# A mixture-of-experts layer on Trainium2: expert results scatter-added into the output in memory instead of stored as parts and summed in a last stage

## The reference, cut to what matters

```
h = layernorm(x) * (1 + cb) + sb
logits = h @ router_w.T;  topk_w, topk_idx = top_k(softmax(logits), 2);  topk_w /= sum(topk_w)
for e in range(8):
    out += (silu(h @ Wg[e].T) * (h @ Wu[e].T)) @ Wd[e].T * comb[:, e]
x = x + gb * out          # gb: one row of 256 gates per batch
```

## Time and profile before

| what | us |
|---|---|
| median of 3 runs | 319.98 |
| lowest and highest | 319.64, 322.03 |
| the profiled execution, own time | 321.41 |
| the profiled execution, span from first to last instruction | 319.6 |
| mean granted TensorE clock (share of full speed) | 0.873 |

### The profile page before, as it was taken

The page is one execution under the profiler, slowest core; times in us unless marked ns, Lnnn a source line. Parts: engine busy times, 40 slices in busy tenths (PEclk is TensorE's granted clock), DMA queues, the critical chain, the costliest instruction groups (busy, mean ns, idle before and its releaser), DMA issues.

```text
span 319.6 us, 4248 instructions
## 1 busy us (share of the span) xinstructions
PE 248.6 (78%) x1154; PEld 157.7 (49%) x1155; DVE 170.7 (53%) x448; ACT 119.7 (37%) x262; POOL 82.5 (26%) x93
## 2 busy tenths in 40 slices
PE   3889298967452228999997899999999999999500
PEld 0236166656352113666664466666666666666300
DVE  1356805798877972844667244444444444443236
ACT  1158367427828243564453222223232323222000
POOL 0103646531100051022242122223333222211223
PEclk9999859997555556999999799999999999999955
DMA  7993270418072925231011111011010111100083
GB/s 266 362 417 127 71 295 33 180 25 352 2 257 105 301 69 207 91 126 29 33 36 33 33 33 35 21 36 33 17 45 29 33 34 44 33 2 0 0 269 125
DMA packets 12663, 33.88 MB, mean 106 GB/s; under 512 B 2049, under 2 KB 7684, under 8 KB 11624
## 3 DMA queue, kind: packets, MB, share of 16 engines
q1 hardware_dynamic: 10152, 28.51, 24.5%
q0 software_dynamic: 2208, 5.17, 5.5%
q10 hardware_dynamic: 288, 0.02, 0.1%
HBM read 29.45 MB, written 5.14 MB: 108 GB/s over the span
## 4 chain that ended last, share of the span: by engine, by line
PE 68%; DVE 18%; DMA 5%; ACT 4%; issue 3%; SPq 1%; POOL 0%; DVEq 0%; POOLq 0%; ACTq 0%
PE bank L572 27%; PE bank L600 19%; PE bank L584 5%; PE bank L464 4%; PE bank L501 2%; DVE W L873 2%; ACT W L646 2%; PE bank L421 2%; DMA W<-expert_parts 2%; PE bank L477 2%; PE bank L561 2%; DMA x<-in_x 2%; PE bank L489 1%; DMA rows<-token_rows,source_i 1%; PE bank L533 1%
## 5 line engine op out<-in xcount | busy, mean ns | idle before, releaser
L572 PE MATMUL bank<-W,rows 128*128 x414 | 90.2, 374 | 4.2 <-DVE W L873 3.2
L600 PE MATMUL bank<-W,shared 128*128 (+1 forms) x276 | 67.9, 388 | 0.7 <-DVE shared L1067 0.7
L572 PEld LDWEIGHTS bank<-W,rows 128*128 128x128 f16 x414 | 41.6, 101 | 46.8 <-issue 10.4
L1043 DVE SCALAR_TENSOR_TENSOR shared<-bank,unscale,rows 128x256 f32<-128x256 f32 (+1 forms) x69 | 31.7, 461 | 60.7 <-ACT rows L723 56.2
L1142 POOL DMA_INDIRECT expert_parts<-shared,dest_i x23 | 23.3, 1014 | 131.4 <-DVE shared L1052 131.4
L600 PEld LDWEIGHTS bank<-W,shared 128*128 128x128 f32 (+1 forms) x276 | 48.7, 189 | 13.4 <-issue 8.6
L723 ACT ACTIVATE rows<-bank,unscale 128x256 f32<-128x256 f32 (+1 forms) x69 | 31.4, 455 | 51.8 <-PE bank L572 40.9
L1128 POOL DMA_INDIRECT rows<-token_rows,source_i x23 | 25.7, 1118 | 34.9 <-DVE source_i L843 28.2
L646 ACT ACTIVATE W<-staged,w_scale_bits 128x704 f16<-128x704 f32 x32 | 25.9, 870 | 11.7 <-DVE w_scale_bits L863 11.7
L733 ACT ACTIVATE shared<-bank 128x128 f32<-128x128 f32 x23 | 6.4, 277 | 62.1 <-PE bank L584 62.1
L873 DVE SCALAR_TENSOR_TENSOR W<-staged,w_scale_bits,W 128x704 f16<-128x704 f32 x32 | 29.4, 966 | 0.0
(11 more groups left out here) (155 smaller groups left out, 255.6 us busy)
## 6 DMA issues: line engine op xcount, KB each, us to landing
staged<-in_w SPq DMA_DIRECT2D x8, 1408.0 KB, 6.4
W<-in_w SPq DMA_DIRECT2D x8, 768.0 KB, 8.8
W<-expert_parts SPq DMA_DIRECT2D x8, 256.0 KB, 4.8
W<-in_wmod SPq DMA_DIRECT2D x3, 512.0 KB, 7.4
token_rows<-rows SPq DMA_DIRECT2D x1, 1040.0 KB, 5.8
x<-in_x SPq DMA_DIRECT2D x4, 256.0 KB, 8.8
W<-mod_rows SPq DMA_DIRECT2D x4, 256.0 KB, 4.4
out<-x SPq DMA_DIRECT2D x4, 256.0 KB, 2.3
```

The costliest lines, as they stand in the source:

```text
L572: mm = pe.matmul(bank[2 + n][:, 0:2 * w], slot[:, kc * P:(kc + 1) * P], W1_pairs[:, bass.ds(e * 2 + part, 1), :, kc, n * PIECE:n * PIECE + w],
L600: mm = pe.matmul(bank[7][:, 0:D], actT[0:rows, fc * P:(fc + 1) * P], W2[0:rows, bass.ds(e * W2_EXP + fc * D, D)], start=(fc == 0), stop=(f ...
L1043: ve.scalar_tensor_tensor(act[:, n * PIECE:n * PIECE + w], bank[2 + n][:, w:2 * w], unscale[c % 2][:, 1:2], sig[:, n * PIECE:n * PIECE + w ...
```

## The change

Each expert result is multiplied by weight and gate in one VectorE instruction and is then added, by the DMA itself, to the output in memory, which has been filled with the residual `x` beforehand. In detail:

1. The rows of `token_rows` grow from 260 to 516 numbers: behind each token's row stands its batch's gate row (`GATE`). SP writes these four gate blocks from `gate_b` early on, behind a new wait on `gateb_in`. The gathers fetch 516 numbers per slot. Two of the four buffers `xs` now lie in `rows1`, two in `x`.
2. SP writes `x` to `out` (four transfers of 256 KB) once the second normalization is done. POOL's first gather waits for this and for the gate blocks, besides the old waits.
3. `result` becomes a `scalar_tensor_tensor` with the gathered gate as second operand.
4. The scatter goes to `out` with an addition, and each waits until the scatter before it has landed, since two results of one token add to the same row. `out` has 128 rows more: an empty slot of partition p adds to row 1024 + p, and nothing is out of bounds any more. VectorE computes `pad_row` for that.
5. The reload of the parts, `finish` and the four output transfers at the end are gone. The kernel ends when all scatters have landed.

```diff
-        rows_d = nc.dram_tensor("token_rows", (TOKENS, ROW), F32, kind="Internal").ap()
-        parts_d = nc.dram_tensor("expert_parts", (2 * TOKENS, D), F32, kind="Internal").ap()
+        rows_d = nc.dram_tensor("token_rows", (TOKENS, ROW_ALL), F32, kind="Internal").ap()
...
-        xs = [rows1[:, r * ROW:(r + 1) * ROW] for r in range(4)]
+        xs = [rows1[:, r * ROW_ALL:(r + 1) * ROW_ALL] for r in range(2)] + [x[:, r * ROW_ALL:(r + 1) * ROW_ALL] for r in range(2)]
...
+            sp.wait_ge(s["gateb_in"], 16 * B)
+            for b in range(B):
+                gate = gate_b[:, b * (D + 1):b * (D + 1) + D].rearrange("p (a d) -> p a d", a=1)
+                sp.dma_start(rows_d[b * S:(b + 1) * S, GATE:].rearrange("(t p) n -> p t n", p=P),
+                             gate.to_broadcast([P, TB, D])).then_inc(s["gates_out"], 16)
             load_w2(2)
             load_w2(3)
...
+            sp.wait_ge(s["h2_ok"], B)
+            for b in range(B):
+                sp.dma_start(out[b * S:(b + 1) * S].rearrange("(t p) d -> p t d", p=P),
+                             v3(x[:, b * TB * D:(b + 1) * TB * D], TB)).then_inc(s["x2_out"], 16)
             sp.wait_ge(s["rows_ok"], 1)
-            sp.dma_start(rows_d.rearrange("(t p) n -> p t n", p=P), v3(rows1[:], TT)).then_inc(s["rows_out"], 16)
+            sp.dma_start(rows_d[:, 0:ROW].rearrange("(t p) n -> p t n", p=P), v3(rows1[:], TT)).then_inc(s["rows_out"], 16)
...
+            sp.wait_ge(s["x2_out"], 16 * B)
             for r in range(2):
                 sp.wait_ge(y_out[r], 16 * len(range(r, SLOT_TILES, 2)))
-            for b in range(B):
-                for k, part in enumerate((part1, part2)):
-                    sp.dma_start(v3(part[:, b * TB * D:(b + 1) * TB * D], TB),
-                                 parts_d[k * TOKENS + b * S:k * TOKENS + (b + 1) * S].rearrange("(t p) d -> p t d", p=P)
-                                 ).then_inc(part_in[b], 16)
...
+            ve.tensor_scalar(pad_row[:], keep[:, C_TOKEN:C_TOKEN + 1], float(TOKENS), None, ALU.add)
...
-            ve.tensor_scalar(nobody[:], filled[:], 0.5, float(NOWHERE), ALU.is_lt, ALU.mult)
+            ve.tensor_scalar(nobody[:], filled[:], 0.5, pad_row[:, 0:1], ALU.is_lt, ALU.mult)
...
-            link(ve.tensor_tensor(nobody[:], nobody[:], filled[:], ALU.add))
+            link(ve.tensor_tensor(nobody[:], nobody[:], source[:], ALU.add))
...
-                ve.tensor_scalar(y_sb[r], bank[7][:, 0:D], slot_weight[c % 4][:, 0:1], None,
-                                 ALU.mult).then_inc(s["y_ok"], 1)
+                ve.scalar_tensor_tensor(y_sb[r], bank[7][:, 0:D], slot_weight[c % 4][:, 0:1], xs[c % 4][:, GATE:],
+                                        ALU.mult, ALU.mult).then_inc(s["y_ok"], 1)
...
             po.wait_ge(s["rows_out"], 16)
+            po.wait_ge(s["gates_out"], 16 * B)
+            po.wait_ge(s["x2_out"], 16 * B)
             po.wait_ge(s["source_ok"], 1)
...
                 po.wait_ge(s["y_ok"], j + 1)
-                po.indirect_dma_start(parts_d, bass.IndirectOffsetOnAxis(dest_i[:, j:j + 1], 0), y_sb[r], None,
-                                      bounds_check=last_part, oob_is_err=False).then_inc(y_out[r], 16)
+                if j:
+                    po.wait_ge(y_out[1 - r], 16 * ((j + 1) // 2))
+                po.indirect_dma_start(out, bass.IndirectOffsetOnAxis(dest_i[:, j:j + 1], 0), y_sb[r], None,
+                                      bounds_check=last_row, oob_is_err=True, compute_op=ALU.add).then_inc(y_out[r], 16)
```

More of the change, by code:

```diff
@@ L26 @@
 WEIGHT, WEIGHT_STEP, UNSCALE = D, D + 1, D + 2
-NOWHERE = 1 << 20
+GATE = ROW
+ROW_ALL = ROW + D
 PIECE = 256
@@ L238, in layer @@
         dest_i = sb("dest_i", NT, U32)
+        pad_row = sb("pad_row", 1)
         slot_weight = [sb(f"slot_weight{r}", 1) for r in range(4)]
@@ L272, in layer @@
             gu_done sig_ok act_ok xt_done slot_hi_ok slot_lo_ok unscale_ok at_done actT_a actT_v down_done y_ok
-            fin_ok pool_fin_ok out_done""".split()
+            gates_out x2_out""".split()
         s = {n: sem(n) for n in names}
@@ L280, in layer @@
         wmod_in = [sem(f"wmod_in{n}") for n in range(3)]
-        part_in = [sem(f"part_in{b}") for b in range(B)]
         def wait_places(eng, e):
@@ L311, in turns @@
                 step(0, j)
-        def finish(eng, batches, link, done):
-            for b in batches:
-                cols = slice(b * TB * D, (b + 1) * TB * D)
-                eng.wait_ge(part_in[b], 32)
-                link(eng.tensor_tensor(part1[:, cols], part1[:, cols], part2[:, cols], ALU.add))
-                g3 = gate_b[:, b * (D + 1):b * (D + 1) + D].rearrange("p (a d) -> p a d", a=1).to_broadcast([P, TB, D])
-                link(eng.tensor_tensor(v3(part1[:, cols], TB), v3(part1[:, cols], TB), g3, ALU.mult))
-                eng.tensor_tensor(x[:, cols], part1[:, cols], x[:, cols], ALU.add).then_inc(done, 1)
         block = ctx.enter_context(nc.Block())
@@ L388, in _ @@
             load_w1(7)
+            sp.wait_ge(s["x2_out"], 16 * B)
             for r in range(2):
                 sp.wait_ge(y_out[r], 16 * len(range(r, SLOT_TILES, 2)))
-            for b in range(B):
-                for k, part in enumerate((part1, part2)):
-                    sp.dma_start(v3(part[:, b * TB * D:(b + 1) * TB * D], TB),
-                                 parts_d[k * TOKENS + b * S:k * TOKENS + (b + 1) * S].rearrange("(t p) d -> p t d", p=P)
-                                 ).then_inc(part_in[b], 16)
-            for b in FINISH_DVE[:-1] + FINISH_POOL + FINISH_DVE[-1:]:
-                if b in FINISH_POOL:
-                    sp.wait_ge(s["pool_fin_ok"], FINISH_POOL.index(b) + 1)
-                else:
-                    sp.wait_ge(s["fin_ok"], FINISH_DVE.index(b) + 1)
-                sp.dma_start(out[b].rearrange("(t p) d -> p t d", p=P),
-                             v3(x[:, b * TB * D:(b + 1) * TB * D], TB)).then_inc(s["out_done"], 16)
-            sp.wait_ge(s["out_done"], 16 * B)
         @block.tensor
@@ L1073, in _ @@
             result(0, SLOT_TILES - 1, (SLOT_TILES - 1) % 2)
-            ve.wait_ge(s["gateb_in"], 16 * B)
-            finish(ve, FINISH_DVE, link, s["fin_ok"])
         @block.gpsimd
@@ L1131, in _ @@
             last_token = po.to_reg(TOKENS - 1)
-            last_part = po.to_reg(2 * TOKENS - 1)
+            last_row = po.to_reg(TOKENS + P - 1)
             po.wait_ge(s["rows_out"], 16)
+            po.wait_ge(s["gates_out"], 16 * B)
+            po.wait_ge(s["x2_out"], 16 * B)
             po.wait_ge(s["source_ok"], 1)
@@ L1141, in _ @@
                 po.wait_ge(s["y_ok"], j + 1)
-                po.indirect_dma_start(parts_d, bass.IndirectOffsetOnAxis(dest_i[:, j:j + 1], 0), y_sb[r], None,
-                                      bounds_check=last_part, oob_is_err=False).then_inc(y_out[r], 16)
+                if j:
+                    po.wait_ge(y_out[1 - r], 16 * ((j + 1) // 2))
+                po.indirect_dma_start(out, bass.IndirectOffsetOnAxis(dest_i[:, j:j + 1], 0), y_sb[r], None,
+                                      bounds_check=last_row, oob_is_err=True, compute_op=ALU.add).then_inc(y_out[r], 16)
                 if j + 4 < SLOT_TILES:
                     gather(j + 4)
-            po.wait_ge(s["gateb_in"], 16 * B)
-            finish(po, FINISH_POOL, klink, s["pool_fin_ok"])
 _ORDER = ["L0_attn_X", "L0_attn_W_in", "L0_attn_b_in", "L0_attn_W_out", "L0_attn_b_out", "L0_ffn_router_w",
@@ L1163 @@
     args = [nc.dram_tensor(f"in_{n}", a.shape, F32, kind="ExternalInput").ap() for n, a in arrays.items()]
-    out = nc.dram_tensor("out", (B, S, D), F32, kind="ExternalOutput").ap()
+    out = nc.dram_tensor("out", (TOKENS + P, D), F32, kind="ExternalOutput").ap()
     layer(nc, *args, out)
     r = run_bass_kernel_spmd(nc, [{f"in_{n}": a for n, a in arrays.items()}], core_ids=[0])
-    return r.results[0]["out"]
+    return r.results[0]["out"][:TOKENS].reshape(B, S, D)
```

3 lines of the change are left out of this document (removed).

## The result

The changed kernel takes 308.73 us (median of 4 runs, 308.24 to 309.24) against 319.85 for the kernel before in the same comparison: a ratio of 0.9638 of the means, 95% interval 0.9593 to 0.9682, so 10.2 to 13.0 us less. Forecast were 306.6 us and a range of 303.5 to 314. Direction and range held; the forecast point was 2.1 us too low. The profiled execution's own time is 308.24, its span 306.4.

The account below looks back on a forecast made before the run. The prediction took PE to bound the steady part and the last stage the end. Last scatter issued at 301.8, landing 4.0 and closing 0.4 gave span 306.2, 13.4 less; median 306.6 us, range 303.5 to 314.

Parts of the forecast that it names:

- Removed, 15.9 us: End of the kernel: reload, `finish` and output transfers, from 303.28 to 319.2, all on the path, would be saved.
- 0.4 us of closing: End of the kernel: only 0.4 us would follow the last scatter's landing.
- nothing else covers it: End of the kernel: no other work would hide the removed last stage, so its whole 15.9 us would be saved.
- L = 4.0: Adding scatter, issue to landing: 2.1 us plain, 1.3 for a round trip, 0.6 for more bytes.
- The upper bound of 12.5: Adding scatter's issue-to-landing time if each DMA engine took its 8 rows singly, 1.3 us each on top of 2.1.
- The waits, 0: Between scatters: waiting for the earlier landing costs nothing, until landing takes 7.4 us, or 4.52 at the last two.
- First gather, 0.5: Front of the kernel: the first gather, widened to 516 numbers, comes 0.5 us later, bounds 0 and 1.0.
- Gate transfers, 0: Early SP queue: waiting for gates delays down weights 2 and 3 by 6 to 9 us, at no cost.
- Residual to `out`, 0: Before the tiles: writing 1 MB delays ACT's weights 4.0 us, covered by 8.85 us of idling; cost 0, bounds 0 and 3.
- 3: Rival at the front: the residual's 1 MB delays weights or first gather by up to 3 us; median up to 309.6; chance 0.04.
- 1: Rival at the end: landing takes 4.5 to 7.4 us, last two scatters in series; median up to about 313; chance 0.20.
- 2: Rival in the tiles: landing over 7.37 us makes scatters the chain, losing from 7.9, median up to 426; chance 0.10.

Follow-up runs that it names:

- the doubled scatters: Changed kernel with each adding scatter issued twice, the second after the first has landed; ratio 1.0639 against the kernel before, span 339.5 us.
- the memset: Changed kernel with one more POOL instruction at its end, a 128 x 1 memset waiting for the last landing in buffer 0; ratio 0.9712 against the kernel before.

## Why the prediction was right or wrong, point by point

- **Removed, 15.9 us.** As a stretch of the chain it was right; as a saving it was not. It was worth 13.3, shown by the kernel before without its stage. This is the step that failed, in the form "0.4 us of closing" and "nothing else covers it": in the trace of before that 0.4 followed a landing at which POOL had finished its drain, though only by 0.9 us. I carried it over to an end at which POOL works until the last moment. There the time from the last landing to the end was 2.2 us. What a deleted stage covers has to be asked of each engine, the end-of-program instructions included.
- **L = 4.0.** Measured 3.8 (3.7 for the last scatter), but not from the parts that I added. The plain scatter of the same wait structure took 2.4 and not 2.1, and the addition 1.4 more and not 1.9; of these 1.4, 0.57 are descriptors, a term that I had put at nothing. The round trip of 1.3 was not measured by itself. So the closeness is in part luck. The upper bound of 12.5, rows one after another in each DMA engine, is far off. From the last issue to the end it is 5.85 where I had 4.0 + 0.4. This one term is 1.45 us of the 2.1 by which the median lies over the forecast. L entered the result less than in the forecast: 1.4 us more of landing moved the end by 0.8. By the fit above, an estimate, it moves the end only from about 3.5 on, and then one for one.
- **The Trainium skill** (Collectives: The Full Stack, "Why ReduceScatter is half of AllGather") counts twice the reads for an addition. My estimate from that alone, L = 2.4, does not agree with the trace: 3.8. The packets of the transfer took more than three times as long in sum as those of the plain scatter (the view adds up packet times, so its share can exceed 1). In windows of half a microsecond in the changed kernel:

```profile
302.50:303.00 0.50, 0.00 (x0) 0.00 (x0) 0.00 (x0) 0.00 (x0) 0.00 (x0) 0.50 0.76 68
303.00:303.50 0.50, 0.00 (x0) 0.00 (x0) 0.00 (x0) 0.00 (x0) 0.00 (x0) 0.50 1.12 156
303.50:304.00 0.50, 0.00 (x0) 0.00 (x0) 0.00 (x0) 0.00 (x0) 0.00 (x0) 0.50 0.28 39
```

  (0.76 + 1.12 + 0.28) x 0.5 = 1.08 us of packet time per engine for one scatter, against 0.32 for the plain one in the earlier trace rows. "Three times the bytes" in my estimate would be 0.96, so this part was about right.
- **The waits, 0.** Right but for the 0.05 us at the last scatter, by the kernel without them. The thresholds were wrong, for the 0.77 us between a landing and the next issue: 6.6 and not 7.4 in the steady part, 3.75 and not 4.52 at the end.
- **First gather, 0.5.** Measured 0.57.
- **`result`, 0.** Right: 482 ns against 484. `pad_row`: about the 0.1 allowed.
- **Gate transfers, 0.** SP waited 4.0 us for the gate broadcasts and issued the four at 43.79, down weights 2 and 3 at 45.82; gate and up weights 2 went out at 57.23, held by VectorE as before.
- **Residual to `out`, 0.** ACT's wait for the staged weights grew from 1.15 to 3.28 us, so by 2.1 where I had allowed 4.0; its idle time ahead of the next work fell from 8.85 to 6.87. No wait followed on PE:

```profile
101.22 1.38 ACT L620 ACTIVATE W<-staged 128x1408 bf16<-128x1408 f32 x1 [3.28 <-DMA staged<-in_w]
...
114.01 3.20 ACT L628 ACTIVATE W<-staged,w_scale_bits 128x704 f16<-128x704 f32 x4 [6.87 <-DVE w_scale_bits L846]
```

- **The rest of the 2.1 us** is the reference point. The forecast carried the difference between two spans over to the medians. The spans did differ by 13.2 (13.4 forecast) for partly wrong reasons: the profile of before came 1.4 us above its median, and that of the changed kernel was the fastest of its four.
- **The rivals.** 3 did not occur. Of 1 there is only the 0.05 us at the last scatter, with L = 3.8 just past the edge. 2 did not occur, but its mechanism is real: the doubled scatters show it.

## What to carry to other kernels

A stage at the end of the chain is worth its length less whatever ran beside it unseen; look for the engine whose end-of-program instruction comes last once the stage is gone. With dozens of indirect DMAs issued by GpSimd that instruction takes microseconds, and a drain placed in an idle gap of GpSimd, shortly before the end, takes most of it off the path. An adding scatter with serial waits is free while its landing plus 0.8 us fits under the step it lies beside (here 4.6 under 7.37, but no longer under the 4.52 of the last two), and doubling it is a cheap test of how far that is from the edge.

## What the runs showed of the hardware that was not expected

- **GpSimd's final drain grows with the number of indirect DMAs**: 4.1 to 4.3 us from its last work to the end with 46, 5.9 with 69, and 2.6 (hardly more than the landing) with 3 or 2 left after an earlier drain. That its time counts from GpSimd's last work, whatever this is, is shown by the memset; that it also cannot end before the last landing, and ends later the more DMAs there were, is read from the table of drains and was not tried. Nor was what it works off.
- **An adding scatter of 128 rows of 1 KB** costs GpSimd 1.55 to 1.6 us instead of 1.0, lands 3.8 us after its issue instead of 2.4, and has 1.08 us of packet time per DMA engine instead of 0.32.
- **The first part scatters by several microseconds with TensorE's clock.** The first gather was issued between 113.4 and 118.1 us. In the nine profiles with a granted clock of 1.00 from 23 to 33 us it came at 115.01 or before, in the five with 0.66 to 0.83 at 116.86 or after. In the changed kernel it came at 114.36, with the memset at 117.61. Columns as in the earlier trace rows; the changed kernel first:

```profile
23.00:33.00 10.00, 9.20 (x37) 6.37 (x38) 6.23 (x15) 7.25 (x17) 4.20 (x6) 1.00 0.35 143
```

```profile
23.00:33.00 10.00, 10.00 (x26) 6.62 (x26) 3.89 (x13) 5.81 (x13) 1.95 (x4) 0.68 0.34 140
```

  26 matmuls instead of 37 in the same ten microseconds. Differences below 1% between versions of this kernel are therefore only readable from distances inside a profile, not from spans.
